# The new cell of an LSTM step is kept in SBUF by a ScalarE copy from PSUM instead of a second VectorE computation

## The reference, cut to what matters

```python
xW = jnp.einsum('ntd,dg->ntg', x, Wx) + b
def step(carry, xw_t):
    prev_h, prev_c = carry
    a = xw_t + prev_h @ Wh
    i = jax.nn.sigmoid(a[:, :Hdim])
    f = jax.nn.sigmoid(a[:, Hdim:2 * Hdim])
    o = jax.nn.sigmoid(a[:, 2 * Hdim:3 * Hdim])
    g = jnp.tanh(a[:, 3 * Hdim:])
    next_c = f * prev_c + i * g
    next_h = o * jnp.tanh(next_c)
    return ((next_h, next_c), next_h)
return x + hs
```

## Time and profile before

| | |
|---|---|
| median of 3 runs | 1846.87 us (1845.93 to 1848.51) |
| profiled execution, its own time | 1846.18 us |
| its span | 1844.4 us |
| TensorE's granted clock, mean | 0.998 of full speed |
| PE matmul busy | 1689.8 us, 92% |
| DVE busy | 1724.7 us, 94% |
| ACT busy | 1013.6 us, 55% |
| POOL busy | 174.8 us, 9% |

### The profile page before, as it was taken

One profiled execution on the slowest core, in us unless ns is written; L12 is line 12 of the kernel. 1 busy time (PEld: TensorE's weight loads), 2 busy tenths in 40 slices (PEclk: granted clock), 3 DMA queues, 4 the chain that ended last, 5 costly groups with the idle time before them and its releaser, 6 DMA issues.

```text
span 1844.4 us, 105808 instructions
## 1 busy us (share of the span) xinstructions
PE 1689.8 (92%) x45212; PEld 1087.2 (59%) x45212; DVE 1724.7 (94%) x10378; ACT 1013.6 (55%) x3992; POOL 174.8 (9%) x539
## 2 busy tenths in 40 slices
PE   6999999999999999999999999999999999999997
PEld 4565555565555556555555655555665555565555
DVE  8999999999999999999999999999999999999998
ACT  5555555555555555555555555555555555555554
POOL 1000000000000000000000000000000000000000
PEclk9999999999999999999999999999999999999999
DMA  5000000000000000000000000000000000000000
GB/s 212 20 21 21 25 23 21 21 26 21 21 25 22 21 21 26 21 21 26 21 21 21 27 21 21 26 21 21 21 26 21 21 24 23 21 21 26 18 12 15
DMA packets 39065, 49.02 MB, mean 27 GB/s; under 512 B 4416, under 2 KB 36160, under 8 KB 38592
## 3 DMA queue, kind: packets, MB, share of 16 engines
q1 hardware_dynamic: 37152, 37.77, 6.6%
q10 hardware_dynamic: 1440, 4.49, 0.6%
HBM read 25.46 MB, written 16.78 MB: 23 GB/s over the span
## 4 chain that ended last, share of the span: by engine, by line
DVE 67%; PE 22%; ACT 8%; issue 3%; DMA 1%; ACTq 0%; DVEq 0%
DVE turned L600 22%; PE acc L386 13%; DVE mailbox L604 13%; DVE products L613 11%; PE acc L392 8%; ACT gates L305 7%; DVE h_halves L628 4%; DVE h_halves L639 4%; DVE gates L622 2%; DVE x_tops L681 2%; DVE h_feat L633 2%; DVE mailbox L618 2%; DVE out_ring L668 2%; DVE x_halves L584 1%; DMA wx<-in_wx 1%
## 5 line engine op out<-in xcount | busy, mean ns | idle before, releaser
L386 PE MATMUL acc<-wh_low,h_halves 128*32 128x256 f16 x16384 | 719.7, 274 | 135.3 <-DVE h_halves L628 130.8
L392 PE MATMUL acc<-wh_high,h_halves 128*32 128x256 f16 x16384 | 719.7, 274 | 0.0
L386 PEld LDWEIGHTS acc<-wh_low,h_halves 128*32 128x32 f16 x16384 | 391.9, 97 | 394.1 <-DVE h_halves L628 380.4
L378 PE MATMUL x_accs<-wx_high,x_halves 128*32 128x512 f16 x8192 | 620.9, 380 | 1.5 <-ACT x_accs L244 1.5
L305 ACT ACTIVATE gates<-mailbox 128x96 f32<-128x96 f32 x1024 | 256.1, 250 | 640.7 <-DVE mailbox L604 637.6
L600 DVE STREAM_TRANSPOSE turned<-acc 128x256 f32<-128x256 f32 x1024 | 458.1, 447 | 30.4 <-PE acc L392 17.8
L392 PEld LDWEIGHTS acc<-wh_high,h_halves 128*32 128x32 f16 x16384 | 350.7, 95 | 105.5 <-issue 0.2
L378 PE MATMUL x_accs<-wx_low,x_halves 128*32 128x512 f16 x4096 | 398.8, 379 | 0.0
L248 ACT ACTIVATE acc<-x_accs,masks 128x512 f32<-128x512 f32 x511 | 334.1, 654 | 0.0
L215 POOL TENSOR_TENSOR o_preact<-turned 128x32 f32<-128x32 f32 x512 | 165.6, 324 | 1650.5 <-DVE turned L600 1650.5
L613 DVE SCALAR_TENSOR_TENSOR products<-gates 128x64 f32<-128x64 f32 x1024 | 231.3, 226 | 61.4
(11 more groups left out here) (92 smaller groups left out, 569.2 us busy)
## 6 DMA issues: line engine op xcount, KB each, us to landing
out<-out_ring SPq DMA_DIRECT2D x128, 128.0 KB, 2.1
x_ring<-in_x SPq DMA_DIRECT2D x120, 128.0 KB, 3.0
wx<-in_wx ACTq DMA_DIRECT2D x4, 512.0 KB, 8.1
wx<-in_wx SPq DMA_DIRECT2D x4, 512.0 KB, 8.0
wh<-in_wh SPq DMA_DIRECT2D x4, 512.0 KB, 16.8
wh<-in_wh ACTq DMA_DIRECT2D x4, 512.0 KB, 17.1
x_ring<-in_x SPq DMA_DIRECT2D x2, 512.0 KB, 16.6
b_rows<-in_b ACTq DMA_DIRECT2D x1, 256.0 KB, 21.3
```

The lines of the kernel that those rows point to most:

```text
L378: last = pe.matmul(x_acc[pair % 2][32 * j:32 * j + 32], x_halves[:, pair % (CHUNK // 2), c, half], w[:, c].rearrange("p (n q) g -> p q n g ...
L386: pe.matmul(acc[par][32 * j:32 * j + 32, n, 0:GL], h_halves[1 - par][:, c, 0:2], w_low["wh"][:, c, n * Q + j], start=False, stop=False, sk ...
L392: last = pe.matmul(acc[par][32 * j:32 * j + 32, n, 0:GL], h_halves[1 - par][:, c, 1:3], w_high["wh"][:, c, n * Q + j], start=False, stop=c ...
```

## The change

VectorE's two calls of `keep_cell` go, with the wait on `cell_kept` behind them. ScalarE gets two copies from PSUM (`cell[n]`) to the same SBUF place, behind `tanh_of_cell(1)` and ahead of everything that follows it in ScalarE's queue. Copy n waits until VectorE has written `full_h(n)`, since that instruction reads the same PSUM bank. In step 6 of a chunk the copy of group 1 waits too until VectorE has read `x_sums` (`scale_step`), which lies in the same bank. `add_three(n)` of the next step waits for the copy, and so does TensorE's `x_sums` product. The one semaphore becomes two.

```diff
-        cell_kept = sem("cell_kept")
+        cell_kept = [sem(f"cell_kept{n}") for n in range(NG)]
@@ ScalarE
+                def keep_cell(n):
+                    act.wait_ge(h_feat_ready, NG * t + n + 1)
+                    act.activation(gates[1 - par][n][:, 0, :], cell[n], ACT.Copy).then_inc(cell_kept[n], 1)
+
                 three_gates(0)
                 last_gate(0)
                 three_gates(1)
                 tanh_of_cell(0)
                 last_gate(1)
                 tanh_of_cell(1)
+                keep_cell(0)
+                if at == 6 and chunk + 1 < CHUNKS:
+                    act.wait_ge(scale_step, 5 * chunk + 7)
+                keep_cell(1)
                 if chunk == 0 and at in (0, 1):
                     high_of_x(chunk, at + 2)
@@ TensorE
                 if at == 6 and chunk + 1 < CHUNKS:
                     pe.wait_ge(x_top_ready, chunk + 2)
+                    pe.wait_ge(cell_kept[1], t)
                     pe.matmul(x_sums, ones_16[:], x_top[:], start=True, stop=True).then_inc(x_sum_ready, 1)
@@ VectorE
                 def add_three(n):
                     dve.wait_ge(turned_ready, nth[n])
+                    if t > 0:
+                        dve.wait_ge(cell_kept[n], t)
                     dve.tensor_tensor(preact[n], turned[n][:, 0:6, 0, :], turned[n][:, 0:6, 1, :], ALU.add)\
                         .then_inc(preact_ready, 1)
@@
-                def keep_cell(n):
-                    dve.scalar_tensor_tensor(gates[1 - par][n][:, 0, :], products[n][:, 0, :], 0.5, products[n][:, 1, :],
-                                             ALU.mult, ALU.add).then_inc(cell_kept, 1)
@@
                 full_h(0)
-                keep_cell(0)
                 low_of_h(0, 2, 1)
                 high_of_h(1)
                 full_h(1)
-                keep_cell(1)
                 low_of_h(2, 1, 2)
                 low_of_h(3, 1, 2)
-                dve.wait_ge(cell_kept, NG * (t + 1))
```

## The result

| | before | after |
|---|---|---|
| median | 1846.92 us (1845.93 to 1848.51, 4 runs) | 1880.17 us (1878.84 to 1880.47, 4 runs) |
| ratio to before, 95% interval | | 1.0174 (1.0162 to 1.0186) |
| profiled execution: span | 1844.4 us | 1877.1 us |

The change makes the kernel slower, by 1.7% as the ratio gives it; the medians lie 33.25 us apart, which is 1.8%. The forecast was 1875.6 us, with a range from 1867 to 1888.

The account below looks back on a forecast made before the run. It took the chain of turn, add, tanh, products, tanh as the bound, not busy shares. Stalls of 12.8 + 13.6 + 2.2 + 0.1 = 28.7 us on 1846.9 gave 1875.6 us, range 1867 to 1888.

Parts of the forecast that it names:

- What bounds the kernel: Step's chain turn, add, tanh, products, tanh, with VectorE and ScalarE waiting in turn, sets the pace, not busy shares.
- The removal: VectorE's two keep_cell writes lie behind full_h in the shadow of a remaining wait: gain 0, at most 5 us.
- The ordinary step: Copy 1 moves ScalarE's place_bias and fill by 0.53 us, covered by 0.74 us idle ahead of the next tanh: cost 0.
- Step 12: high_of_x moves 0.53 us, VectorE's L584 waits for it, next turn(0) is 0.44 us late; 31 times, 13.6 us.
- Step 6: Copy 1 waits also for x_exponent_of, so the tanh of three gates comes 0.42 us late; 12.8 us together.
- Step 14: high_of_x, place_bias and fill queue on ScalarE; the next tanh is 0.07 us late, 31 times, 2.2 us.
- The added waits: add_three's split-off wait, for cell_kept, is long satisfied: 0, upper bound 5 us, plus at most 1.2 us in step 6.
- Rival C: Waits split the other way; add_three(0) waits for turn(0) separately, up to 0.07 us per step, 36 us, about 1911; chance 8%.
- The rule against the row: Skill's rule, read plainly, gives back each removed VectorE write's whole duration, about 1691 us; rows disagree; chance 1%.

Follow-up runs that it names:

- the kernel with the waits swapped: The changed kernel with add_three's two waits in the other order, first for cell_kept, then for turn; 1953.79 us, ratio 1.0578.
- The removal alone: The kernel before without VectorE's two keep_cell writes and the wait behind them, nothing in their place; 1846.93 us, ratio 0.9996.
- the waits alone: The kernel before, VectorE's keep_cell kept; add_three gets a second wait, for the kept cell, and the wait ahead of the output row goes; 1848.74 us, ratio 1.0007.
- the copies that don't wait: The changed kernel with the tanh of the cell written to SBUF and the copies' wait for full_h dropped; 1870.16 us, ratio 1.0123.

## Why the prediction was right, point by point

**What bounds the kernel**: right. The busy shares of 92% and 94% said nothing of what an instruction is worth: 1024 instructions could go and the time stayed.

**The removal**: predicted 0, measured 0 (0.9996, with 0.9987 to 1.0005).

**The ordinary step**: predicted at no cost, with a shift of 0.53 us under a cover of 0.74. The shift is 0.53, the cover left 0.21 us.

**Step 12**: predicted 0.44 us and 13.6 in all, measured 0.45 (3.96 against 3.51) and 14.1. The stall is the forecast one, but the shift of 0.53 us under it was right partly by luck. The prediction moved high_of_x by the same 0.53 as in an ordinary step and did not ask when the load of the register ahead of it would begin. It began with copy 1. Had it begun with the tanh, as before, high_of_x could have started 0.09 us behind copy 1, only 0.28 us late (0.53 + 0.09 - 0.34), and the stall would be about 0.19 us, an estimate from these rows.

**Step 6**: predicted 0.42 and 12.8 us, measured 0.47 and 14.3. **Step 14**: predicted 0.07 and 2.2 us, measured 0.11 and 3.4. Both terms are small for the same reason: how long a fill holds ScalarE. I took a value between the 0.52 us of place_bias, of the same size, and the 0.57 us of the only fill in the earlier trace rows with work right behind it. The rows of the trace after show 0.57 both times, 1043.09 to 1043.66 and 1071.71 to 1072.28. With 0.57 the two terms are 0.45 and 0.10 us. The row of the very instruction was there, and its neighbour of the same shape should not have pulled it down. The two terms were short by 2.7 of the 4.6 us by which the forecast was low, and 1.8 of these come from that choice.

**The added waits**: predicted 0 with an end of 6 us; 1.0007 (0.9998 to 1.0016) in the kernel that has them alone. Rival C was excluded by the right row: swapping two lines of the source brings it to life. Its price came out right for the wait alone, 35.6 us against 36, but by luck, and it missed the meeting with GpSimd, which doubled it. The 0.07 us were read from step 6, where add_three(1) starts 0.10 us after the end of turn(1), and put down to the split-off wait. In an ordinary step of the kernel before, where add_three(1) has one wait, it is the same 0.10 us:

```profile
1004.61 0.45 DVE L600 STREAM_TRANSPOSE turned<-acc 128x256 f32<-128x256 f32 x1
1005.02 0.23 DVE L613 SCALAR_TENSOR_TENSOR products<-gates 128x64 f32<-128x64 f32 x1
1005.16 0.26 DVE L604 TENSOR_TENSOR mailbox<-turned 128x96 f32<-128x96 f32 x1
```

gate_products(0) (L613) stands between the two in VectorE's queue, and add_three(1) starts 0.14 us behind it in step 6 as in all others. So that row says nothing of a split-off wait. What one costs was first shown by the kernel with the waits swapped, at add_three(0), which has nothing between it and turn(0).

**The rule against the row.** The Trainium skill, "VectorE: DVE Perf Modes", section "The DRAIN you can't avoid", says that the next operation does not start until the pipeline is empty. In the plain reading of the prediction a removed operation would then save its time. The removal alone shows no saving in this chain (0.9996), where VectorE waits for its own results and for ScalarE.

**Still open**: why an added wait comes with four single steps that are 0.3 us longer. They have the same numbers (133, 190, 450, 488) in the traces of the change and of the kernels built on it, and others in that of the waits alone. What causes them was not tried.

## What to carry to other kernels

Before an instruction is taken off a busy engine, find what the one behind it waits for: if that wait ends no sooner, the instruction was free, whatever the busy share says. Before it is given to an idle engine, find the time at which it may start there, since everything queued behind it moves to that time; then look through all phases of the loop, not an average one, for the place where the queue has less slack than that. Where it must be done, put the work that others wait for ahead of the waiting instruction, and of two users of one PSUM bank let the one that is ready first go first. And before a gap is put down to a wait, look at the same place in a step that does not have that wait.

## What the runs showed of the hardware that I had not expected

- Of an instruction's two waits on VectorE the later one in program order becomes an instruction of its own (1022 in the trace after, and as many with the waits swapped). Satisfied, it costs nothing that the times can tell from zero (1.0007, 0.9998 to 1.0016). If it is the one that ends last, add_three(0) starts 0.10 us after turn(0) has ended instead of 0.03.
- Two sums on VectorE and GpSimd that read the same SBUF tile at once: the one that begins second is slowed. GpSimd's takes 0.32 us when VectorE's began first (mean 324 ns in the page before) and 0.25 when it began first or add_three(0) had ended; VectorE's takes 0.27 when it begins first or alone, and 0.35 when second. The Trainium skill, "GPSIMD Engine Reference", section "Specifications", says that GpSimd's SBUF interfaces are shared with VectorE and contended for by VectorE instructions with two SBUF inputs, of which this sum is one; that fits. That the later one pays, and 0.07 to 0.08 us, is what these traces show.
- A fill from PSUM to PSUM of 128x512 holds ScalarE's queue 0.57 us, a place_bias of the same size from SBUF to PSUM 0.52, though both end later than that (0.65 and 0.60 us).
- A register load on ScalarE (0.28 us) began 0.01 us after the last waiting instruction ahead of it had begun, and ran beside that one and those behind it: with the tanh of group 1 in the kernel before and with the copies that don't wait, with the waiting copy 1, 0.54 us after the tanh, in the changed kernel.
